# Heads loop: the maximum, difference and exponential of a chunk's scores moved from the end of a step to the head of the next

## The reference

```python
h = x @ Wm + bm
t = h.reshape(bs * L_ * H, HD)               # 8 heads of 32 per token
logits = t @ expert_emb                      # 16 experts per head
w = jax.nn.softmax(logits, axis=-1)
topw, topi = jax.lax.top_k(w, K)             # K = 2
hmid = gelu(einsum('td,edi->tei', t, W1) + b1); eo = einsum('tei,eio->teo', hmid, W2) + b2
out = (the two chosen eo, weighted by topw, summed) @ Wo + bo
```

## Time and profile before

| what | us |
| --- | --- |
| three runs | 2375.44, 2378.33, 2393.04 (median 2378.33) |
| span of the profiled execution, the only time noted of it | 2466.2 |
| of it the steps with early routing, from the maximum in step 13 to that of the last chunk | 136.24 |
| of it the expert stage | 911 |
| busy in the whole span: PE, DVE, ACT, POOL | 2088.2 (85%), 1331.5 (54%), 1290.4 (52%), 818.1 (33%) |

### The profile page before, as it was taken

How to read it: one execution, slowest core, us unless ns; L and a number is a source line. 1 busy time by engine, 2 the same in 40 slices (tenths; PEclk the granted TensorE clock), 3 DMA queues, 4 the chain that set the end, 5 groups by cost and what they waited for, 6 DMA issues and landing times. The chain is left out here.

```text
span 2466.2 us, 36023 instructions
## 1 busy us (share of the span) xinstructions
PE 2088.2 (85%) x12850; PEld 1155.0 (47%) x12851; DVE 1331.5 (54%) x2117; ACT 1290.4 (52%) x1634; POOL 818.1 (33%) x608
## 2 busy tenths in 40 slices
PE   6998699997975653788289887799999999999998
PEld 3444355554544442577155554344444444444443
DVE  5666435554555554122166675366666766666633
ACT  2444222222542221122134342698989989988997
POOL 4332211120005554000657511234434334334343
PEclk8999779998996665899578896899999999999999
DMA  2010211212523331576323311555565655556554
GB/s 54 27 34 8 85 59 59 69 55 85 198 89 107 104 100 43 161 209 198 95 64 114 105 59 60 143 162 158 163 162 153 163 155 159 159 160 163 155 151 117
DMA packets 280563, 281.24 MB, mean 114 GB/s; under 512 B 44998, under 2 KB 261654, under 8 KB 280278
## 3 DMA queue, kind: packets, MB, share of 16 engines
q1 hardware_dynamic: 246422, 233.49, 33.8%
q0 software_dynamic: 12288, 25.72, 3.5%
q10 hardware_dynamic: 21696, 19.93, 2.4%
HBM read 203.76 MB, written 75.25 MB: 113 GB/s over the span
## 5 line engine op out<-in xcount | busy, mean ns | idle before, releaser
L2326 ACT ACTIVATE BIG<-psA,b_s 128x1024 f32<-128x1024 f32 x784 | 809.8, 1116 | 89.8 <-PE psA L2265 82.2
L2254 POOL TENSOR_TENSOR BIG<-BIG 128x1024 f32<-128x1024 f32 x147 | 359.6, 2446 | 553.1 <-DVE BIG L2347 553.1
L2265 PE MATMUL psA<-x_r,w_r 128*128 128x512 f32 x1568 | 480.4, 427 | 20.4 <-DMA x_r<-hs_d 12.2
L2347 DVE SCALAR_TENSOR_TENSOR BIG<-psY,b_s,BIG 128x512 f32<-128x512 f32 x392 | 291.6, 749 | 247.6 <-PE psY L2275 246.8
L2265 PEld LDWEIGHTS psA<-x_r,w_r 128*128 128x128 f32 x1568 | 269.0, 190 | 330.5 <-ACT BIG L2326 244.9
L2275 PE MATMUL psY<-BIG,w_s 128*32 128x512 f32 x3136 | 400.9, 602 | 2.9 <-DVE BIG L2347 2.2
L1199 POOL DMA_INDIRECT xg_d<-xnb,SLOT x128 | 131.6, 1028 | 144.2 <-issue 75.4
L719 DVE TENSOR_REDUCE b_nm<-psN 112x32 f32<-112x512 f32 x128 | 83.1, 686 | 148.3 <-PE psN L616 147.8
L1774 POOL DMA_INDIRECT gath<-yg_d,SLOT x128 | 129.9, 1015 | 83.8 <-issue 42.9
L2275 PEld LDWEIGHTS psY<-BIG,w_s 128*32 128x32 f32 x3136 | 73.6, 108 | 160.9 <-issue 91.3
L719 DVE TENSOR_REDUCE a_nm<-psN 98x32 f32<-98x512 f32 x128 | 82.3, 685 | 90.8 <-PE psN L607 90.6
(11 more groups left out here) (394 smaller groups left out, 3242.9 us busy)
## 6 DMA issues: line engine op xcount, KB each, us to landing
BIG<-wt_d SPq DMA_DIRECT2D x784, 128.0 KB, 3.2
x_r<-hs_d SPq DMA_DIRECT2D x196, 128.0 KB, 3.5
xg_d<-ex SPq DMA_DIRECT2D x64, 264.0 KB, 3.6
xv<-xg_d SPq DMA_DIRECT2D x66, 256.0 KB, 3.1
BIG<-ypad_d SPq DMA_DIRECT2D x140, 120.0 KB
xv<-x SPq DMA_DIRECT2D x64, 196.0 KB, 2.6
hs_d<-xv SPq DMA_DIRECT2D x32, 392.0 KB
yg_d<-ex ACTq DMA_DIRECT2D x33, 256.0 KB, 3.6
```

The costliest lines, as they stand in the source:

```text
L2254: eng.tensor_tensor(gacc[:, w % 2], gacc[:, w % 2], gsum[:, a % 2], ALU.add).then_inc(Q["acc"], 1)
L2265: mm = eng.matmul(psA[m % 3][:, b * BLK:(b + 1) * BLK], w1_r[:, m % 16], x_r[:, w % 2, b * BLK:(b + 1) * BLK], start=True, stop=True)
L2326: eng.activation(hid[:, m % 8], psA[m % 3][:], ACT.Gelu, bias=b1_s[:, m % 16:m % 16 + 1]).then_inc(Q["gel"], 1)
L2347: eng.scalar_tensor_tensor(out=dst, in0=psY[use % 2][:], scalar=b2_s[:, g % 4:g % 4 + 1], in1=wb[:, g % 3, b * BLK:(b + 1) * BLK], op0=ALU ...
```

## The change

In the heads loop `choose` and `weights_exp` of chunk c are called at the head of step c+7 instead of at the end of step c+6, and the loop's range is one step longer on DVE and ACT.

```diff
@@ block.vector
-                for s in range(1, T + 7):
+                for s in range(1, T + 8):
+                    if live(s - 7):
+                        choose(s - 7)
                     if live(s - 6):
                         normalise_2(s - 6)
...
                     if live(s - 1):
                         add_experts(s - 1)
-                    if live(s - 6):
-                        choose(s - 6)
...
@@ block.scalar
-                for s in range(1, T + 7):
+                for s in range(1, T + 8):
+                    if live(s - 7):
+                        weights_exp(s - 7)
                     if live(s - 1):
                         weigh_first(s - 1)
...
                     if live(s - 5):
                         inverse_2(s - 5)
-                    if live(s - 6):
-                        weights_exp(s - 6)
```

## The result

The changed kernel takes 2364.72 us (median of six runs, 2350.44 to 2369.94) against 2381.34 for the kernel before (six runs, 2375.44 to 2393.04). The ratio is 0.9917, with a 95% interval of 0.9892 to 0.9942: 20 us less, between 14 and 26. A second timing, beside other runs of the kernel before, gave 0.9896 (0.9864 to 0.9928). The forecast was 0.5% less, the measured change is 0.8 to 1.0%: the direction and the place were right, the sum of 11.7 us was too small.

A forecast was written before the change was run, and what follows sets the result against it. In steps with routing work, PE, the busiest engine, was taken to wait for DVE's routing between the logits and `linear`. Eight step gains summed to 11.7 us, taking the median 2378.33 to 2366.6 us (value 2367), range 2353 to 2379.

The forecast's parts named there:

- the sum of 11.7 us: Heads loop, steps 13 to 20: predicted gains of all eight steps added up, 11.7 us less time.
- The mechanism of the waits: Heads loop, steps 13 to 20: routing moves into DVE's idle time before `choose`, so PE waits less before `linear`.
- steps 13, 17 and 18: DVE idles longer than routing needs, so PE's own queue binds; PE's waits of 0.59, 1.73 and 1.40 us go.
- The 19.7 us for all of PE's waits: Steps 13 to 20: largest possible gain, all of PE's wait before `linear` and the two transposes, 19.7 us.
- Steps 14, 15 and 19: DVE's idle time before `choose` is shorter than routing, so DVE still binds; gains 1.25, 1.25 and 1.55 us.
- Steps 16 and 20: Transposes stop waiting for routing, `choose` follows `route_copy`; `linear` starts 1.07 and 2.89 us earlier.
- rival B: Steps 13 to 20: PE's clock rises as its waits shorten, 16 us on top, 2351 us; chance 0.13.
- C: Heads loop: the gain is given back by waits elsewhere in the step, time stays about 2378 us; chance 0.13.
- D: Steps 13 to 20: shifted PE pauses lower the clock, 16 us lost against 11.7 gained, 2383 us; chance 0.11.
- The rule on the most-contended engine: PE, not DVE, is busiest in the heads loop; by occupancy alone reordering DVE gives nothing, 2378 us.
- A: Steps 13 to 20: the summed waits alone, 9 to 15 us less, 2363 to 2369, value 2367 us; chance 0.63.
- the stated range: Whole kernel time: 2353 to 2379 us, covering all of A and C and the near part of rival B.

The follow-up runs named there:

- more_after: The changed kernel with four more routing-sized DVE instructions per step in steps 7 to 12, ahead of `choose`; 0.9919 of the kernel before.
- more_before: The kernel before with four more routing-sized DVE instructions per step at the end of steps 7 to 12, behind `choose`; 1.0079 of the kernel before.
- short_before: The kernel before with the heads loop's 32 routing instructions each replaced by a one-column write, order kept; 0.9877 of the kernel before.
- late_choose: The changed kernel with `choose` moved further, behind `deviation_1` on DVE, and `weights_exp` behind `square_1` on ACT; 0.9918 of the kernel before.

## Why the prediction was too small

**The mechanism of the waits was right.** Only steps 13 to 20 move, on DVE alone; the routing goes into DVE's idle time; `choose` behind `route_copy` costs nothing net; PE's idle time in R, which ends with ACT's work for the most part, is 12.0 us before and 12.6 after; the expert stage starts 12 us after the last logits in either kernel and keeps its time (the 911 us of the earlier trace rows are 906 to 910 from its first matmul to the end in all three profiles of either kernel). more_after against more_before shows the waits with the work put elsewhere. In all, PE's idle time fell by 10.7 us where the sum had 11.7. What the sum lacks is that the same matmuls of PE took 8.6 us less.

**The step that failed is the one for steps 13, 17 and 18.** It holds PE's clock, and with it PE's and DVE's idle times, as they were in one profile. Segment G, predicted (the first profile before, less the term) and measured in three profiles after:

| step | before, three profiles | term | predicted | after, three profiles |
| --- | --- | --- | --- | --- |
| 13 | 6.50, 6.77, 5.15 | 0.59 | 5.91 | 3.82, 3.81, 3.81 |
| 14 | 4.82, 4.82, 5.75 | 1.25 | 3.57 | 3.94, 4.99, 5.02 |
| 15 | 5.15, 5.15, 5.15 | 1.25 | 3.90 | 2.97, 3.81, 3.81 |
| 16 | 6.37, 6.39, 6.38 | 1.07 | 5.30 | 5.04, 5.03, 5.04 |
| 17 | 5.16, 5.16, 5.15 | 1.73 | 3.43 | 2.94, 2.39, 2.39 |
| 18 | 4.83, 4.83, 4.83 | 1.40 | 3.43 | 3.22, 2.39, 2.39 |
| 19 | 5.16, 5.15, 5.15 | 1.55 | 3.61 | 5.17, 3.81, 3.81 |
| 20 | 6.74, 6.74, 6.73 | 2.89 | 3.85 | 3.52, 3.21, 3.21 |
| sum | 44.7, 45.0, 44.3 | 11.7 | 33.0 | 30.6, 29.4, 29.5 |

In those three steps I let PE's own queue bind, at the length that it had in that profile: the idle time of 0.59, 1.73 and 1.40 us was the most that could go. But PE ran at its low level there for all or most of G (granted clock 0.57, 0.64 and 0.50), and its length was no property of the step. After the change the clock of G was 1.00 in steps 13 and 17 in all three profiles and in step 18 in two, and there `linear` waits for DVE (0.7 us after step 13, 1.1 and 0.6 after 17, 0.6 after 18), where the prediction had no idle time. Segment G of step 17 in the second profile before, then G and R behind it in the third profile before and after (columns as in the earlier trace rows):

```profile
1390.84:1396.00 5.16, 3.43 (x8) 1.61 (x7) 4.98 (x9) 0.63 (x1) 0.00 (x0) 0.65 0.25 78
```

```profile
1398.80:1403.95 5.15, 1.82 (x6) 0.89 (x6) 4.98 (x9) 0.63 (x1) 0.00 (x0) 1.00 0.26 81
1403.95:1418.38 14.43, 12.40 (x48) 8.30 (x48) 5.79 (x13) 3.76 (x10) 2.68 (x2) 0.62 0.15 56
```

```profile
1390.86:1393.25 2.39, 1.82 (x6) 0.90 (x7) 2.32 (x5) 0.63 (x1) 0.00 (x0) 1.00 0.03 7
1393.25:1404.68 11.43, 9.40 (x48) 6.23 (x48) 8.10 (x17) 3.76 (x10) 2.68 (x2) 0.85 0.31 105
```

In the kernel before, G is 5.15 us in step 17 whether its clock is 0.65 or 1.00, because DVE fills it (4.98 us of work): at full clock PE simply idled longer, 3.33 us instead of 1.73.

```profile
1403.95 4.26 PE L2070 MATMUL ps<-xv,wm_s 128*128 128x392 f32 x7 [3.33 <-DVE xv L1854]
```

With the routing gone from it, G is what `choose` and `normalise_2` need, 2.39 us, in steps 17 and 18 of the two later profiles. In the first, 0.6 us of routing is left behind the logits of step 17 (G 2.94), and PE is at the low level in step 18 (0.50, G 3.22). In step 13 the logits come so early that 1.5 us of routing is left behind them in each profile. So step 17 was worth 2.6 us and not 1.73, step 18 2.2 and not 1.40, step 13 2.3 and not 0.59 (means of three profiles each): together 3.4 us more than the three terms. These were upper bounds by the clock of one profile; what DVE still has to do behind the logits bounds them without it. The 19.7 us for all of PE's waits were no bound on the time for the same reason: the two timings gave 20 and 25.

Steps 14, 15 and 19, where I had DVE bind, gave 0.5, 1.6 and 0.9 us in the mean against 1.25, 1.25 and 1.55: 1.1 less than predicted. After the change PE ran at the low level in step 14 of two profiles. In step 19 of the first one nothing is gained: PE had done R of step 18 in 7.83 us at full clock, against 9.26 in the later two, and its logits were ready before DVE began the routing, 0.1 us later. Steps 16 and 20 gave 4.8 against 4.0.

**The rest, 4.5 us of R, is rival B's, and its cause is open.** No work of R is moved, and PE's idle time in it hardly changes; its length follows the clock. The higher clock in G of steps 13, 17 and 18 belongs to B as well. The forecast gave a rising clock 0.13, because a wait of 1.69 us had stood at full clock. The table shows the clock higher wherever the routing is hidden or shrunk in all eight steps, and the timed runs agree (0.911 against 0.906), which is more than chance would do. The obvious reason, PE's pauses, was tried and is not settled: with a part of them filled the clock was 0.78. The three profiles before have the clock of step 13's G at 0.57, 0.57 and 1.00. The Trainium skill (TensorE: Matmul & The Clock Gate, Part 1) has activity release the clock, and the moment of it vary from run to run: the three profiles agree with the second, and that activity in this wait raises the clock no run here shows.

**The rivals.** C took 0.6 us at most, PE's added idle time in R, and D did not occur: the clock rose. The rule on the most-contended engine (the Trainium skill, Perfetto Trace Analysis, Identifying Performance Opportunities), read by occupancy alone, gave 2378: here a reordering on an engine with 82 of 136 us busy was worth 20 us, since it shortened the waits of PE, the busiest one.

**What was too sure.** The measured 20 us lie outside A's 9 to 15; the stated range held them because it took in the near part of B. The chance of faster by over 1% was put at 0.08. The two ratios lie at 0.8 and 1.0%, with intervals that reach beyond 1%.

## What to carry to other kernels

In a step whose end waits for two engines, cut it at the instruction that both lead to and write down each engine's own length of work in between; the gain of shortening one is bounded by the other's length, and both must be taken at the clock that PE can have, not at the one that it happened to have in one profile. Work that nobody waits for in the same step belongs ahead of the instruction that waits, not behind it: here the early routing cost 26 us behind it and 3 to 7 ahead (medians, against short_before). And moving a piece once more can hand the wait to the next reader: after a gain in one segment, look at the segment behind it before the edit is called free.

## What the runs showed of the hardware

Steps with the same instructions repeat between executions to hundredths of a microsecond, with the clock's pattern in them: R of steps 13 to 20 in the first two profiles before differs by 0.06 us at most in each step (11.54 and 11.54, 14.81 and 14.80, 12.87 and 12.93, and so on), while another profile differs by some us in single steps. And semaphores are not all that holds one engine against another: DVE is slower beside some work of POOL. In the three profiles of either kernel the addition L1842 takes 1.42 to 1.47 us wherever POOL's subtraction in the splitting of the heads (L1783) does not run, also beside the gathers (L1774), and 2.86 to 4.22 us in the 11 places where it does, in step 19 of every profile among them. `weigh_second` (L1798) in late_choose, 3.69 us against 1.66, is the same.
